# A three-stage FFN, attention, FFN kernel: its hand-written order is changed at the starts, seams and leads

## What is computed

```python
x = x + 0.5 * ffn(layernorm(x))        # stage 1
x = x + attention(layernorm(x))        # stage 2: 16 heads of 32, 8 key heads, rotary, tanh cap, causal
x = x + 0.5 * ffn(layernorm(x))        # stage 3

def ffn(inp):
    x = w_norm * inp * rsqrt(mean(inp * inp) + eps)
    w_topk, sel = top_k(softmax(x @ w_router), 4)      # 4 of 32 experts, at most 128 tokens each
    y = (silu(buf @ w_gate) * (buf @ w_up)) @ w_down    # buf: tokens of each expert, F = 176
    sh = silu(x @ sw_gate) * (x @ sw_up) @ sw_down      # shared expert, F = 704
    return inp + scatter_add(y * w_topk) + sigmoid(x @ w_shared_gate) * sh
```

## Time and profile before

| | us |
|---|---|
| median of 3 runs | 955.45 (955.0 to 955.5) |
| the profiled execution, whole | 955.5 |
| its span, first to last instruction | 953.8 |
| PE busy | 910.6 |
| DVE busy | 694.7 |
| ACT busy | 531.3 |
| POOL busy | 507.6 |

### The profile page before, as it was taken

One profiled execution on the slowest core, in us unless ns is written; L12 is line 12 of the kernel. 1 busy time (PEld: TensorE's weight loads), 2 busy tenths in 40 slices (PEclk: granted clock), 3 DMA queues, 4 the chain that ended last, 5 costly groups with the idle time before them and its releaser, 6 DMA issues.

```text
span 953.8 us, 18310 instructions
## 1 busy us (share of the span) xinstructions
PE 910.6 (95%) x6274; PEld 683.3 (72%) x6274; DVE 694.7 (73%) x1704; ACT 531.3 (56%) x793; POOL 507.6 (53%) x537
## 2 busy tenths in 40 slices
PE   3999999999999999999999999988999999999997
PEld 2788887777778765666666666557888877777786
DVE  5988778554444779989998999978887785544435
ACT  5766653132233478878887888866666531322322
POOL 6243203555552477887888788834431135555530
PEclk9999999999999999999999999999999999999999
DMA  6343218777774510011001002004432177777725
GB/s 201 105 140 98 71 42 225 178 174 185 180 181 115 157 66 24 22 34 33 22 22 44 22 11 87 15 12 128 128 110 71 42 222 168 185 180 184 177 41 170
DMA packets 95433, 101.91 MB, mean 107 GB/s; under 512 B 18688, under 2 KB 86656, under 8 KB 95360
## 3 DMA queue, kind: packets, MB, share of 16 engines
q1 hardware_dynamic: 83072, 83.17, 28.4%
q0 software_dynamic: 12288, 17.83, 11.0%
HBM read 65.44 MB, written 35.54 MB: 106 GB/s over the span
## 4 chain that ended last, share of the span: by engine, by line
PE 44%; DVE 13%; issue 4%; ACT 3%; POOL 2%; DVEq 0%; POOLq 0%; ACTq 0%
PE zT L1013 4%; PE gu L87 4%; PE gu L88 3%; PE gu L89 3%; PE gu L1033 3%; PE pj_at L87 3%; PE pv_at L1667 3%; PE pj_at L89 3%; PE pj_at L88 3%; PE scores_at L1651 2%; PE down L87 2%; PE down L88 2%; PE down L89 2%; PE den_at L1683 2%; DVE turned_at L1903 2%
## 5 line engine op out<-in xcount | busy, mean ns | idle before, releaser
L87 PE MATMUL gu<-x_hi,gu_hi 128*128 128x512 f32 x264 | 120.7, 457 | 1.2 <-DVE act_gu L1287 1.1
L786 POOL DMA_INDIRECT rows<-z_rows,slots x64 | 68.0, 1062 | 73.2 <-DVE slots L1278 54.3
L1763 ACT ACTIVATE capped_at<-scores_at 128x2048 f32<-128x2048 f32 x64 | 93.2, 1456 | 22.1 <-PE scores_at L1651 21.8
L89 PE MATMUL gu<-x_lo,gu_hi 128*128 128x512 f32 x264 | 103.9, 394 | 0.0
L88 PE MATMUL gu<-x_hi,gu_lo 128*128 128x512 f32 x264 | 103.7, 393 | 0.0
L1092 ACT CAST a_hi<-act_gu 128x512 fp32r<-128x512 f32 x96 | 59.1, 616 | 80.0 <-DVE act_gu L1287 63.3
L1771 ACT ACTIVATE probs_at<-capped_at 128x2048 f32<-128x2048 f32 x64 | 95.2, 1487 | 2.5
L87 PE MATMUL down<-down_hi,a_hi 128*128 128x256 f32 x300 | 93.9, 313 | 0.0
L1168 ACT ACTIVATE y<-gu,rows 128x256 f32<-128x256 f32 x64 | 30.3, 474 | 109.6 <-PE gu L1033 64.8
L1840 POOL TENSOR_SCALAR_AFFINE_SELECT probs_at<-probs_at 128x1024 f32<-128x1024 f32 x64 | 85.4, 1340 | 9.8 <-ACT probs_at L1771 9.2
L1013 PE MATMUL zT<-w_gu,xT 128*128 128x352 f32 x256 | 86.3, 460 | 0.0
(11 more groups left out here) (250 smaller groups left out, 2592.4 us busy)
## 6 DMA issues: line engine op xcount, KB each, us to landing
w_gu<-in_w_gate SPq DMA_DIRECT2D x64, 176.0 KB
w_gu<-in_w_up SPq DMA_DIRECT2D x64, 176.0 KB
w_down<-in_w_down SPq DMA_DIRECT2D x64, 176.0 KB
z_rows<-z SPq DMA_DIRECT2D x16, 512.0 KB, 3.0
acc<-base SPq DMA_DIRECT2D x10, 512.0 KB, 3.2
out<-base SPq DMA_DIRECT2D x10, 512.0 KB, 3.3
xn_at<-acc SPq DMA_DIRECT2D x16, 256.0 KB, 2.7
x<-xn_at SPq DMA_DIRECT2D x16, 256.0 KB, 2.1
```

The lines of the kernel that those rows point to most:

```text
L87: nc.tensor.matmul(out, w_hi, x_hi, start=first, stop=False)
L89: return nc.tensor.matmul(out, w_hi, x_lo, start=False, stop=last)
L786: pool.indirect_dma_start(out=gathered_rows[:, n, :], out_offset=None, in_=m.z_rows, in_offset=bass.IndirectOffsetOnAxis(ap=slots[:, e:e + ...
L1763: nc.scalar.activation(capped[:, u % 2, :, 0:n], scores[:, :, 0:n], ACT.Tanh, scale=QK_SCALE / SOFTCAP).then_inc(capped_ready, 1)
```

## The change

- Lists: list 3 goes to the bank `gu[2]` too, `find(3)` and `list_experts(3)` move from expert 0 into `lead`, the later ones one place forward. `turn_rows(0)` and `copy_rows(0)` leave `lead`, where two pieces stood behind them, and stand directly ahead of the expert loop.
- Slot 3: the down projection runs its tiles j in order, each with all six steps, where j = 0 and 2 first ran five steps and their last step afterwards.
- Start: POOL casts `down_hi` ahead of `scales(1)`; ACT casts and DVE subtracts three of the up splits ahead of `x_hi_parts(0)` and `x_lo_parts(0)`; PE's waits on the splits are simplified.
- Attention, slot 0: POOL makes both parts of the output weights behind its slot; before, POOL made `o_hi` ahead of its first `causal`, and DVE `o_lo`. `causal(0, 2)` goes behind `rope_sum(1, 1)`.
- Slots 14 and 15: `scales(0)` goes behind `rope_sum(15, 0)`; the variances of block 0 go to the start of DVE's slot 14; `denominators` stand ahead of score unit 1; `make_z(0)` is in one piece; `x_hi_parts(0)` goes behind `cap(15, 2)` and `x_lo_parts(0)` behind `take_values(15, 0)`.
- `slot_behind`: `count(f)` and `router(r)` go one chunk forward, `top_experts(f)` ahead of `statistics(s)` and the last residual, `top_experts(r)` ahead of `product(0, 3)`.

```diff
@@ -579,3 +579,3 @@
 
-            bank = gu[2] if r == 1 else small
+            bank = small if r % 2 == 0 or r >= 4 else gu[2]
             return bank[:].rearrange("p (n t) -> p n t", t=P)
@@ -809,4 +809,4 @@
                 make_base(0)
-                front.scales(pool, 1)
                 weights.high_down(pool)
+                front.scales(pool, 1)
                 make_base(1)
@@ -862,3 +862,3 @@
                 reached(pe, in_tile_ready, 1)
-                at_least(pe, lists_ready, r if r > 2 else r - 1)
+                at_least(pe, lists_ready, r if r > 4 else r - 1)
                 for n in range(4):
@@ -872,3 +872,3 @@
                     if weights and b == 0:
-                        reached(pe, weights.lo_made, c // 2 + 1 if c % 2 == 0 and c < GU - 1 else MT + c // 2 + 1)
+                        reached(pe, weights.lo_made, MT + c // 2 + 1)
                     behind = 3 if b < MERGED else 2
@@ -930,12 +930,6 @@
                     turn(s)
-                if s is None:
-                    for mts in (range(MT - 1), range(MT - 1, MT)):
-                        for j in (0, 2):
-                            down_proj(b, j, mts)
-                    down_proj(b, 1, range(MT))
-                    tile_starts()
-                    down_proj(b, 3, range(MT))
-                else:
-                    for j in range(TJ):
-                        down_proj(b, j, range(MT))
+                for j in range(TJ):
+                    if s is None and j == TJ - 1:
+                        tile_starts()
+                    down_proj(b, j, range(MT))
                 if s is not None:
@@ -958,9 +952,8 @@
                 turn(r)
-                chunk(0, 4)
                 count(f)
-                chunk(0, 5)
+                chunk(0, 4)
                 router(r)
-                chunk(0, 6)
+                chunk(0, 5)
                 turn_logits(r)
-                for c in range(7, GU):
+                for c in range(6, GU):
                     chunk(0, c)
@@ -991,6 +984,6 @@
                 find(2)
-                for p in range(10, LEAD - 2):
+                for p in range(10, 14):
                     piece(p)
-                turn_rows(0)
-                for p in range(LEAD - 2, LEAD):
+                find(3)
+                for p in range(14, LEAD):
                     piece(p)
@@ -1029,3 +1022,3 @@
                 if e == 0:
-                    reached(pe, lists_ready, 2)
+                    reached(pe, lists_ready, 4)
                 at_least(pe, y_scaled, e)
@@ -1046,2 +1039,3 @@
             lead()
+            turn_rows(0)
             for e in range(E):
@@ -1055,4 +1049,4 @@
                 piece(last_piece)
-                if e < 10 and e % 2 == 0:
-                    find(3 + e // 2)
+                if e < 8 and e % 2 == 0:
+                    find(4 + e // 2)
                 down_expert(e)
@@ -1176,5 +1170,5 @@
                 make_z(0)
-                weights.high_gate_up(act, MT, MT + 1)
+                weights.high_gate_up(act, MT, MT + 3)
                 x_hi_parts(0)
-                weights.high_gate_up(act, MT + 1, 2 * MT)
+                weights.high_gate_up(act, MT + 3, 2 * MT)
                 take_logits(0)
@@ -1366,5 +1360,5 @@
                 product(0, 0)
-                statistics(s)
-                before.vector_last_residual(dve)
                 top_experts(f)
+                before.vector_last_residual(dve)
+                statistics(s)
                 x_lo_parts(r)
@@ -1377,4 +1371,4 @@
                 weigh(f)
-                product(0, 3)
                 top_experts(r)
+                product(0, 3)
                 a_lo_part(0, 2)
@@ -1403,6 +1397,6 @@
                 list_experts(2)
-                for p in range(13, LEAD - 1):
+                for p in range(13, 17):
                     followup(p)
-                copy_rows(0)
-                followup(LEAD - 1)
+                list_experts(3)
+                followup(17)
 
@@ -1452,4 +1446,5 @@
                 statistics(1)
+                weights.low_gate_up(dve, MT, MT + 3)
                 x_lo_parts(0)
-                weights.low_gate_up(dve, MT, 2 * MT)
+                weights.low_gate_up(dve, MT + 3, 2 * MT)
                 weights.low_down(dve)
@@ -1459,2 +1454,3 @@
             lead()
+            copy_rows(0)
             for e in range(E):
@@ -1469,4 +1465,4 @@
                 followup(last_piece)
-                if e < 10 and e % 2 == 0:
-                    list_experts(3 + e // 2)
+                if e < 8 and e % 2 == 0:
+                    list_experts(4 + e // 2)
             for p in range(behind_experts, LAST_PIECE + 2):
@@ -1706,3 +1702,3 @@
                 weighted_values(b - 1, 1 - q, 3)
-            if following and not ahead:
+            if following:
                 pe.wait_ge(v_copied, SEQS)
@@ -1714,7 +1710,5 @@
                 project(b + 1, 1 - q, 1)
-            if behind and not following:
+            if behind:
                 denominators(b - 1, 1)
             score_unit(b, q, 1)
-            if following:
-                denominators(b - 1, 1)
             if ahead:
@@ -1791,5 +1785,2 @@
                 y_hi_part(b - 1, 0)
-            if not ahead:
-                act.wait_ge(roped_ready, (SEQS - 1) * PIECES + 2)
-                following.x_hi_parts(0)
             cap(b, 1)
@@ -1798,5 +1789,6 @@
                 normalise(b + 2, held)
-            elif ahead:
-                following.make_z(0, range(0, 2))
             cap(b, 2)
+            if not ahead:
+                act.wait_ge(roped_ready, (SEQS - 1) * PIECES + 2)
+                following.x_hi_parts(0)
             if behind and ahead:
@@ -1811,3 +1803,3 @@
                 if following:
-                    following.make_z(0, range(2, TJ))
+                    following.make_z(0)
             if further:
@@ -1846,7 +1838,2 @@
                 root(b + 2)
-            elif following:
-                following.front.scales(pool, 0)
-            if isinstance(b, int) and b == 0:
-                pool.wait_ge(ffn_stored, 1)
-                pool.tensor_copy(o_hi[:], m.o[:]).then_inc(o_hi_ready, 1)
             causal(b, 0)
@@ -1855,8 +1842,8 @@
             rope_sum(b + 1, 1 - q, 0)
-            rope_sin(b + 1, 1)
-            if isinstance(b, int) and b == 0:
+            if following:
+                following.front.scales(pool, 0)
                 causal(b, 2)
-                rope_sum(b + 1, 1 - q, 1)
-            else:
-                rope_sum(b + 1, 1 - q, 1)
+            rope_sin(b + 1, 1)
+            rope_sum(b + 1, 1 - q, 1)
+            if not following:
                 causal(b, 2)
@@ -1942,2 +1929,4 @@
                 statistics(b + 2)
+            else:
+                following.front.variances(dve, 0, following.front.read(dve, 0, 3))
             turn(b + 1, 0)
@@ -1949,4 +1938,2 @@
             if not behind:
-                dve.wait_ge(o_hi_ready, 1)
-                dve.tensor_tensor(o_lo[:], m.o[:], o_hi[:].bitcast(F32), ALU.subtract).then_inc(o_lo_ready, 1)
                 add_tiles(b, 0)
@@ -1967,4 +1954,2 @@
                 aT_lo_part(b + 2)
-            if reads:
-                following.front.variances(dve, 0, following.front.read(dve, 0, 3))
             divide(b, 0)
@@ -1979,6 +1964,6 @@
             divide(b - 1, 1)
-            dve.wait_ge(roped_ready, b * PIECES + 2)
-            following.x_lo_parts(0)
             y_lo_part(b - 1, 1)
             take_values(b, 0, dve, dve.tensor_copy)
+            dve.wait_ge(roped_ready, b * PIECES + 2)
+            following.x_lo_parts(0)
             add_tiles(b, 0)
@@ -2120,3 +2105,3 @@
             tensor_slot(SEQS - 3, 1)
-            tensor_slot(SEQS - 2, 0, further=False, following=following)
+            tensor_slot(SEQS - 2, 0, further=False)
             tensor_slot(SEQS - 1, 1, ahead=False, further=False, following=following)
@@ -2142,2 +2127,6 @@
             gpsimd_slot(0, 0)
+            pool.wait_ge(ffn_stored, 1)
+            pool.tensor_copy(o_hi[:], m.o[:]).then_inc(o_hi_ready, 1)
+            pool.wait_ge(o_hi_ready, 1)
+            pool.tensor_tensor(o_lo[:], m.o[:], o_hi[:].bitcast(F32), ALU.subtract).then_inc(o_lo_ready, 1)
             with pool.Fori(0, SEQS // 2 - 2) as i:
```

16 lines of the change are left out of this document (8 added, 8 removed).

## The result

The changed kernel takes 965.53 us, the median of 4 runs (965.30 to 966.35), beside 955.23 us for the kernel before (4 runs, 954.37 to 955.50). The ratio is 1.0111, with a 95% interval of 1.0094 to 1.0129. So it is slower by 10.3 us, about twice the +5.0 that I had forecast, and 0.5 us above the top of my range. The profiled execution took 965.7 us.

The account below looks back on a forecast made before the run. PE was taken to bound the kernel, busy 910.6 of 953.8 us, so only changes in its waits count. Terms -0.8 + 3.2 + 1.1 + 1.5 = +5.0 on 955.5 gave 960.5 us, range 956.7 to 965.0.

Parts of the forecast that it names:

- the lists and leads in stage 1: Stage 1's first list and lead end: two waits go, a fourth list delays the copy for turn_rows(1); +1.5 us.
- the order behind the seam: Slot behind attention: moved top experts make PE wait for product(0, 3), +2.9 us, of which +1.2 is left.
- Step 1: Start of stage 1: router slightly later, but PE's wait for product(0, 3) goes; -0.8 us, bounds -1.1 to +0.5.
- the wait at 39.53: Start of stage 1: PE's wait of 1.05 us for product(0, 3) goes entirely; -1.05 us.
- Step 4: Attention's slot 0: later mask, and POOL late by its split of the output weights; +1.1 us, bounds 0 to +3.
- the mask: Attention's slot 0: causal(0, 2) comes later behind rope_sum(1, 1), and PE waits longer for it; +0.9 us.
- Steps 2 and 3: First list and lead end, both FFNs: the fourth list on DVE delays the row copy; together +3.2 us.
- rival (a): Clock falls after the waits in both leads, PE's work there at half speed, +1.7 us each: 963.9 us; chance 0.19.
- step 5: Attention's slots 14 and 15 and the slot behind: PE waits for roped and x_lo_parts(0); +1.5 us, bounds -2.3 to +4.

Follow-up runs that it names:

- e12_best: The kernel before with POOL's cast of down_hi ahead of scales(1) and the change's order in the slot behind attention; ratio 1.0002.
- e1_start: The kernel before with only the change's start of stage 1, the earlier cast of down_hi and the new split orders; ratio 1.0012.
- e14_after_half: The changed kernel with the adds of the even experts' rows left out in both stages; 966.46 us.
- e15_split_o: The kernel before with only o_hi and o_lo made on POOL behind attention's slot 0, the mask order as before; ratio 1.0035.
- e2_lists: The kernel before with only the change's lists, leads and slot 3 down projection order, in both FFNs; ratio 1.0037.
- e7_mask: The kernel before with only rope_sum(1, 1) ahead of causal(0, 2) in attention's slot 0, the split of o as before; ratio 1.0011.

## Why the prediction was half right

The forecast was 960.5 us with a range up to 965.0, and 965.53 was measured.

**What held.** The sign, and the account of the lists and leads in stage 1: no wait for the ranks at `tile_starts`, none at `find(0)`, a wait of 0.61 in slot 3 (I had 0.9), 2.20 ahead of the second `turn_rows` (I had 1.7), +1.5 in all as forecast. That the sum fits is in part luck: the wait was 0.5 us longer, and slot 3 with the first list gave 0.3 to 0.5 back where I had 0.1. In the seam the waits for `roped` (1.35, forecast 1.1) and for `x_lo_parts(0)` (+2.2 on `output(14)`, forecast +1.7) stand where I had put them; +1.9 against +1.5. That this sum fits is luck too: the order behind the seam, which I had as +1.2 to +2.9 ahead of the slack, was a gain by itself (-0.8; -0.2 in `e12_best`, which has the same edit), and the clock's fall behind `output(14)`, which I had not counted, took part of its place.

**Step 1 failed: 2.2 of the 5.3 us missed.** The failing sentence is "Three subtractions of about 0.35 us fit in that hole". They did not, because the same step had put POOL's cast beside them. I costed each edit by its row of before, where its neighbour on the other engine was another one. The edits apart gave -0.5 and -0.1; together +1.4 in the changed kernel, +0.9 in `e1_start` and +0.6 in `e14_after_half`: how early PE's clock rises at the start differs from execution to execution, so some 0.5 of the 2.2 may be chance. The fault is the same in all three. The other term of the step, -1.05 for the wait at 39.53, was too large as well: the wait went to 0.38 and not to nothing. Most of it belonged to the one execution that I read, where the clock had risen at 20.61 us; in the ten other traces with the old start it rose at 21.4 to 23.3 us and the wait was 0.36 to 0.99 us.

**Step 4 failed by the same fault, 0.7 us.** I had bounded how long POOL's `o_lo` takes (3.22, inside 2.6 to 4.5; 2.35 in `e15_split_o`, below them), and asked only whether POOL comes late for its `root`. It was DVE that came late. And the mask was +0.4 instead of +0.9, since without DVE's `o_lo` beside it POOL's first `rope_sin` took 1.28 us and not 2.23, more than I had taken off; the rest of +1.8 is DVE. The rows of before had the price: DVE's addition of 1024 columns takes 1.21 us in the 13 of its 32 places where POOL is idle beside it, and its median is 2.30. The 1.95 us from which I had worked out 3.9 for `o_lo` on POOL was most likely such a lengthened row.

**Steps 2 and 3 in stage 3: 1.3 us, the clock.** The step had no term for it. My rival (a) came true in one lead of two, as the rows by stretch show above; in `e2_lists` and `e14_after_half` in both. I gave it 0.19 and 1.7 us for a lead; it cost 1.4.

**Not in the prediction:** the 0.7 us at the end of stage 1, which was chance in that one execution. The rest, 0.4 us, is step 5's size.

The range failed because I let each step vary by itself and put the sum of the likely values near its middle, while one fault, engines that hold each other, sat in two steps, and the clock in a third, all with the same sign.

## What to carry to other kernels

When an instruction moves, look up what it now runs beside on DVE and POOL, not only what it was before and behind: two edits that were free apart cost 0.6 to 1.4 us together here. A wait that a change makes can be dearer than its length: behind most waits of 2.06 us or more PE went on at half speed, behind none of up to 1.71 us; so cutting the 2.20 to 1.60 us was worth more than the 0.6. And a wait read in one trace may be that execution's: look at when the clock rose. Where a chain of dependent transfers is nearly as slow as the compute beside it, take it out of both kernels before you compare them.

## What the chip showed that I had not expected

- In these rows DVE waited for the end of POOL's instruction, and not for a share of it: a subtraction of 0.42 us took 1.68 beside a cast, and a scaling of two columns 2.26 instead of 0.17 beside POOL's subtraction, ending with it. An operation with an input in PSUM was not held (1.41 and 1.41), and beside POOL's `rstd_f` of 1.78 us six subtractions were not held either.
- Over the 18 traces, between stage 1's first slot and the end: no fall of the granted clock came with any of 52 PE waits of 1.00 to 1.71 us, and one came within, or up to 1.5 us behind, 25 of 35 waits of 2.06 us or more. The same wait of 2.06 us in the seam came with a fall in 8 traces and without one in 4. The lower level held for 3.4 us, or 6.8 after some of the longer waits.
- In `e7_mask` the fall behind a wait of 2.46 us cost nothing in the end (the shift across the slot is +1.3 right behind the wait, and +1.3 again 10 us later): the kernel before has two waits, 0.72 and 0.36 us, in the next 10 us, which the slow matmuls filled.
- The accumulate transfers took 4.1 us each (median) in one execution and 4.4 in another of the same code; PE's wait at the end of stage 1 was 0.28 to 6.8 us.
